# Source-stationary one-hot touches in a two-layer graph network, with their sums written straight into the layer-1 weight buffers

## The chip, the cores and the metric

The program runs on one core of a Trainium2 chip. The metric is the device time of one execution in microseconds (us), the median of three runs. The core has a matrix engine (PE; PEld is its weight load, which can run beside a matmul), a vector engine (DVE), a scalar engine (ACT), GpSimd (POOL) and a queue engine that issues transfers (SP). On-chip memory (SBUF) has 128 partitions; matmuls write into PSUM, from which ACT or DVE must carry the sums away.

## What is computed

The graph has 2500 nodes and 80000 edges, sorted by target node `dst`; the density of edges falls with the row, since `dst` is drawn as 2500 u². Rows have 1024 columns, all in float32. Two layers follow one another:

```
h = relu(layernorm(x))
s = h @ W0
x = x + segment_sum(s[src] * edge_weight[:, None], dst)            # first graph layer

h = relu(layernorm(x))
g = h @ W1.T + b
row, col = dst and src, with one self loop for each node
deg = number of edges of each row (self loop included)
norm = deg[row] ** -0.5 * deg[col] ** -0.5
out = x + segment_sum(norm[:, None] * g[col], row)                 # second graph layer
```

## The kernel before

Gathers and segment sums are done as dense matmuls. For each tile of 128 target rows the kernel builds a 2500-wide matrix of summed edge weights (20 blocks of 128 sources), and for the second layer a matrix of edge counts. A float32 factor is carried as two float16 parts (high, low), and a product as the three products (0,0), (0,1), (1,0) of parts.

**Touches.** The matrices come from one-hot products. A touch is one matmul over 128 consecutive edges: its stationary side is a one-hot of 128 columns, its moving side a one-hot of the rest of the address, three times (plain, times the weight's high part, times its low part). DVE builds both from fields that POOL copies (L989, L991, L994, L995); eight touches are one step. A window is 4 target rows; four windows are a quad (16 rows), eight quads a tile, 160 quads in all. Before, the stationary side is (row in the window, source block), 4 x 32 = 128 columns, and the moving side the position in the source block, 80 columns times three = 240. Quads 0 to 15 (two tiles) take as many touches as the edges need (352 in 44 steps); quads 16 to 63 take two touches for each window (8 for a quad, 384 in all), quads 64 to 159 one (4 for a quad, 384 in all). A window with edges left over gets further touches; with the edges drawn there are none, before or after.

**Stages.** First the *support* stage: 20 tiles of `h @ W0` (L1634), with transposes (L1617), tables that find each window's edges (L1703) and the touches of the first 16 quads in between. Then the *dense* stage of layer 1: 20 tiles, each 120 matmuls of 512 columns (L1750), cut into eight parts of 15 by `SUMS_AT`; ahead of each part PE does the touches (L1646) of one quad of the tile **two** further on. The last two dense tiles run with no touches. Then layer 2, five chunks of 500 columns: 320 matmuls against the counts (L1846), then four products with `W1` (L1902, 48 matmuls each).

**A quad's way out, before.** ACT makes three copies out of PSUM (L1380 to L1382: the counts in float32, the weights' high part, the low sums); DVE forms the low part (`second_part`, L1054 and L1057); SP stores both parts in DRAM (`store_quad`, L471), ACT's own queue stores the counts (L1384), POOL adds them to a running degree (L741). When a tile's eight quads are stored, SP loads the tile back turned round (`load_weights`, L484, four transposing DMAs of 10 blocks of 128 x 128), two tiles ahead of their use. The counts come back in float32 (`load_counts`, L554); POOL adds the self loops (L787), ACT takes the high part (L1532) and DVE the low (L1221). The degree is summed by PE (L1826) and turned by a DRAM round trip and two PE transposes (L1832, L1833).

**What sets the order.** Each engine has its own program, written out by hand, and waits on semaphores. `win_act`, `win_evac` and `win_lo` say that a quad's ACT copies, the PSUM release and the low part are done, `win_sum` that its counts are added, `agg_ready` that a dense tile is finished. POOL's copies of fields (L734, L735) wait for `hots_ready`, the end of DVE's previous step. SP's queue is in order: a wait there holds all transfers behind it.

## Time and profile before

| | us |
|---|---|
| median of 3 runs | 1483.26 (1482.24 to 1484.04) |
| span of the profiled execution | 1480.6 |
| around the span, to the median | 2.7 |
| PE busy | 1444.0 (98%) |
| DVE / ACT / POOL busy | 958.5 / 441.1 / 303.0 |
| dense matmuls L1750, 2400, busy | 542.2 |
| touches L1646, 1120, busy | 144.2 |
| layer-2 sums L1846, 1600, and products L1902, 960, busy | 339.1 and 209.0 |

A matmul's busy time counts its whole way through a pipelined engine, and matmuls overlap; a group's price is therefore read from the start of one group to the start of the next in the timeline. The chain of waits says which engine the end of the program hangs on. A DMA issue on SP lasts as long as the row says before the next item of SP's queue can go, and lands later.

### The profile page before, as it was taken

Reading aid. Unit: us, or ns where it says so; the run is one execution under the profiler, and the core shown is the slowest. Engines: PE = TensorE matmul, PEld = TensorE weight load, DVE = VectorE, ACT = ScalarE, POOL = GpSimd, SP = SyncE. Lnnn points to the kernel's source line nnn. Section 1 sums busy time; section 2 is a strip of 40 time slices with the busy share of each in tenths; the row PEclk is TensorE's granted clock in tenths of the full one; section 3 lists DMA queues with packets and bytes.
Section 4 is the critical chain, followed back from the end, with each engine's and each line's share of the span. In section 5 each row is a group of like instructions: output and inputs, shape, how many; then the busy total and the mean of one; then the engine's idle time right before and its main releaser. Section 6 shows DMA issues by size and latency. Waiting matters only on the chain.

```text
span 1480.6 us, 24633 instructions
## 1 busy us (share of the span) xinstructions
PE 1444.0 (98%) x7580; PEld 766.2 (52%) x7581; DVE 958.5 (65%) x1732; ACT 441.1 (30%) x869; POOL 303.0 (20%) x578
## 2 busy tenths in 40 slices
PE   3989999999999999999999999999999999999999
PEld 2555555555555555555555544446446446446455
DVE  7788785767877866666665634986554554555542
ACT  7545554422222223322223313812011011021000
POOL 2244333323333333333333310000000000001000
PEclk9999999999999999999999999999999999999999
DMA  8301431237667788888888886804305105104002
GB/s 310 115 24 47 123 102 24 46 80 146 156 149 154 160 180 186 175 182 181 179 183 181 180 181 227 282 29 150 102 8 183 61 18 185 49 29 140 28 1 83
DMA packets 414350, 185.62 MB, mean 125 GB/s; under 512 B 379624, under 2 KB 396540, under 8 KB 414216
## 3 DMA queue, kind: packets, MB, share of 16 engines
q1 hardware_dynamic: 329736, 157.82, 42.0%
q10 hardware_dynamic: 84480, 26.22, 7.2%
q8 instruction: 59, 0.97, 0.3%
q14 instruction: 75, 0.61, 0.2%
HBM read 76.45 MB, written 77.11 MB: 104 GB/s over the span
## 4 chain that ended last, share of the span: by engine, by line
PE 87%; DVE 7%; DMA 2%; issue 2%; ACT 1%; SPq 1%; DVEq 0%; POOL 0%; ACTq 0%; POOLq 0%
PE pair L1750 28%; PE pair L1846 22%; PE pair L1902 13%; PE pair L1634 13%; PE pair L1646 7%; PE pair L1703 1%; PE pair L1617 1%; DVE slots L994 1%; DVE slots L995 1%; DMA h<-x_scratch 1%; DVE negbase L1316 1%; DMA wstage<-c_scratch 1%; DVE slots L989 0%; SPq L484 0%; DVE slots L991 0%
## 5 line engine op out<-in xcount | busy, mean ns | idle before, releaser
L1750 PE MATMUL pair<-h,area 128*128 128x512 f16 x2400 | 542.2, 379 | 0.5 <-issue 0.5
L1750 PEld LDWEIGHTS pair<-h,area 128*128 128x128 f16 x2400 | 233.8, 98 | 252.5 <-issue 2.2
L1846 PE MATMUL pair<-area,h 128*128 128x500 f16 x1600 | 339.1, 374 | 1.3 <-DVE h L1250 1.3
L1846 PEld LDWEIGHTS pair<-area,h 128*128 128x128 f16 x1600 | 155.5, 97 | 184.0 <-issue 2.2
L741 POOL TENSOR_TENSOR deg_acc<-deg_acc,area 128x320 f32<-128x320 f32 x160 | 151.8, 949 | 363.1 <-ACT area L1382 363.1
L1902 PE MATMUL pair<-wmat,area 128*125 128x512 f16 x960 | 209.0, 379 | 0.0
L1380 ACT ACTIVATE area<-pair 128x320 f32<-128x320 f32 x160 | 70.1, 438 | 425.2 <-PE pair L1646 416.6
L1902 PEld LDWEIGHTS pair<-wmat,area 128*125 128x125 f16 x960 | 130.6, 136 | 75.5
L1054 DVE SCALAR_TENSOR_TENSOR area<-pair,area 128x320 f16<-128x320 f32 x160 | 77.6, 485 | 133.6 <-ACT area L1382 112.1
L1646 PE MATMUL pair<-slots 128*128 128x240 f16 x1120 | 144.2, 267 | 7.2 <-DVE slots L995 6.1
L1646 PEld LDWEIGHTS pair<-slots 128*128 128x128 f16 x1120 | 108.8, 98 | 54.2 <-DVE slots L995 11.0
L1564 ACT ACTIVATE area<-pair,sc 128x500 f16<-128x500 f32 x40 | 27.1, 677 | 364.8 <-PE pair L1846 364.8
L1634 PE MATMUL pair<-wmat,agg_t 128*128 128x512 f16 x480 | 112.2, 384 | 3.1 <-DVE wmat L890 3.1
L1301 DVE SCALAR_TENSOR_TENSOR area<-pair,sc,area 128x500 f16<-128x500 f32 x40 | 29.3, 737 | 131.1 <-ACT area L1564 131.0
L1634 PE MATMUL pair<-wmat,xt 128*128 128x512 f16 x480 | 110.7, 382 | 0.0
L989 DVE TENSOR_TENSOR slots<-iota_r,fbuf 128x640 f16<-128x640 f16 x141 | 74.4, 528 | 49.5 <-PE pair L1646 19.6
L991 DVE TENSOR_TENSOR slots<-iota_r,fbuf 128x1024 f16<-128x1024 f16 x141 | 96.3, 683 | 0.0
L1057 DVE TENSOR_TENSOR area<-area 128x320 f16<-128x320 f16 x160 | 78.7, 492 | 5.5
L995 DVE TENSOR_TENSOR slots<-slots,fbuf 128x640 f16<-128x640 f16 x141 | 80.5, 571 | 0.0
L994 DVE TENSOR_TENSOR slots<-slots,fbuf 128x640 f16<-128x640 f16 x141 | 78.0, 553 | 0.0
L1634 PEld LDWEIGHTS pair<-wmat,agg_t 128*128 128x128 f16 x480 | 46.9, 99 | 54.3 <-issue 6.3
L1634 PEld LDWEIGHTS pair<-wmat,xt 128*128 128x128 f16 x480 | 46.7, 99 | 51.7 <-issue 1.8
(240 smaller groups left out, 1171.6 us busy)
## 6 DMA issues: line engine op xcount, KB each, us to landing
c_scratch<-area ACTq DMA_DIRECT2D x160, 160.0 KB, 3.0
a_scratch<-area SPq DMA_DIRECT2D x320, 80.0 KB, 2.4
xt<-in_x SPq DMA_DIRECT2D x19, 512.0 KB, 3.9
x_scratch<-xt SPq DMA_DIRECT2D x19, 512.0 KB, 3.4
xt<-x_scratch SPq DMA_DIRECT2D x20, 448.0 KB
out_x<-xt SPq DMA_DIRECT2D x19, 448.0 KB
wstage<-c_scratch SPq DMA_DIRECT2D x17, 500.0 KB, 4.2
slots<-c_scratch SPq DMA_DIRECT2D x17, 500.0 KB, 5.4
```

The lines of the kernel that those rows point to most:

```text
L741: pool.tensor_tensor(deg_acc[:], deg_acc[:], c_stage(s), ALU.add).then_inc(win_sum, 1)
L989: nc.vector.tensor_tensor(part(hot(s), M0, SB), columns(8, SB), by_touch(s, 1, 8, SB), ALU.is_equal).then_inc(hots_plain, 1)
L991: nc.vector.tensor_tensor(part(hot(s), 0, P), columns(8, P), by_touch(s, 0, 8, P), ALU.is_equal)
L994: nc.vector.tensor_tensor(part(hot(s), W0C, SB), part(hot(s), M0, SB), by_touch(s, 2, 8, SB), ALU.mult)
L995: nc.vector.tensor_tensor(part(hot(s), W1C, SB), part(hot(s), M0, SB), by_touch(s, 3, 8, SB), ALU.mult).then_inc(hots_ready, 1)
L1054: nc.vector.scalar_tensor_tensor(a_stage(s)[:, 1], sums[:, :, SB:2 * SB], A_DOWN, a_stage(s)[:, 0], ALU.mult, ALU.subtract).then_inc(win_e ...
L1057: nc.vector.tensor_tensor(a_stage(s)[:, 1], a_stage(s)[:, 1], a_stage(s)[:, 2], ALU.add).then_inc(win_lo, 1)
L1634: last = pe.matmul(dest[:, half * H:(half + 1) * H], h_t(t)[:, q, k, :], wmat[:, r, k, half * H:(half + 1) * H], start=k == q == r == 0, s ...
L1646: return pe.matmul(dest, touches[:, t, 0:P], touches[:, t, P:CS], start=first, stop=last, skip_group_check=True)
L1750: last = pe.matmul(sum_pair(e)[:, half * H:(half + 1) * H], wts(e)[:, q, k, :], hpart(k, r)[:, half * H:(half + 1) * H], start=k == q == r ...
L1846: ins = pe.matmul(sums_of(c, f), hpart(k, q)[:, f * P:(f + 1) * P], counts, start=first and q == 0, stop=last and q == 1, skip_group_check ...
L1902: last = pe.matmul(out_pair(m)[0:RW, half * H:(half + 1) * H], agg_of(k, q)[:, b * RW:(b + 1) * RW], wmat[:, r, k, half * H:(half + 1) * H ...
```

## The change

The two sides of a touch change places. The stationary side becomes the one-hot of the source's position in its block of 128, and the moving side (row in the window, source block of 20), times three: 120 columns for a window of 2 rows, 240 for a window of 4. Quads 0 to 63 get eight windows of 2 rows, quads 64 to 159 four windows of 4. There are 384 touches (48 steps) for the first 16 quads and 384 for quads 16 to 63, all of 120 columns, then 384 of 240.

The sums now lie with the source position on partitions, as the dense matmuls want their stationary side. ACT and DVE write them directly into the weight buffer of the next tile (`quad_of`); there the block index k runs fastest, so that one stationary operand, `wts(e)[:, q, :, k]`, takes every 20th float16 (40 bytes apart). Only the first two tiles are still parked in DRAM (`park_quad`, `fetch_parked`). The touches run one tile ahead of the dense part instead of two: dense tile 0 and tile 19 run with no touches, and a tile's dense part waits for all its quads (`win_lo`). `SUMS_EARLY` makes the first seven parts of a tile 13 or 14 matmuls and the last 25.

The counts are split at once: POOL adds the self loop into each quad (`add_self`), ACT takes the high part (`counts_first`, now in each quad), POOL the low part (`counts_left`). SP stores both as float16 (`store_counts`), and layer 2 loads them turned round by transposing DMAs, five of 16 blocks and two of 40 blocks of 128 x 128 for each chunk. The degree is reduced by DVE (`deg_turned`), with no PE part. `V_HALF` grows from 288 or 192 extra columns to two halves of 384 in the window tables.

```
         def wts(b):
...
-            return area[:, b * T * P:(b + 1) * T * P].bitcast(f16).rearrange("p (q k d) -> p q k d", q=2, k=T)
+            return area[:, b * T * P:(b + 1) * T * P].bitcast(f16).rearrange("p (q d k) -> p q d k", q=2, k=T)
...
+        SUMS_EARLY = [0, 14, 27, 41, 54, 68, 81, 95, 120]
...
-                nc.vector.tensor_tensor(part(hot(s), M0, SB), columns(8, SB), by_touch(s, 1, 8, SB),
+                n = r * T
+                nc.vector.tensor_tensor(part(to, P, n), columns(8, n), by_touch(s, 0, 8, n),
...
+            def add_self(n, s, td, q):
+                pool.wait_ge(more_consts, 3)
+                pool.wait_ge(win_sum, n + 1)
+                own = by_source(c_stage(s))[:, bass.ds(td, 1), :]
+                pool.tensor_tensor(own, own, half_ident[:, q * RQ:(q + 1) * RQ].unsqueeze(1), ALU.add).then_inc(c_self, 1)
+
+            def counts_left(n, s, first_parts, second_parts):
+                pool.wait_ge(c_hi, n + 1)
+                pool.tensor_tensor(second_parts, by_source(c_stage(s)), first_parts, ALU.subtract).then_inc(c_lo, 1)
...
-                need(act, st_out[s], STORED(n, s))
-                need(act, win_sum, n - 1)
+                need(act, c_lo, n - 1)
+                need(act, win_lo, n - 1)
...
+            def counts_first(n, s, to):
+                act.wait_ge(c_self, n + 1)
+                act.activation(to, by_source(c_stage(s)), ACT.Copy).then_inc(c_hi, 1)
...
+            def store_counts(td, b):
+                sp.wait_ge(c_lo, QPT * td + QH * (b + 1))
+                for z in range(2):
+                    sp.dma_start(c_rows[z][:, :, bass.ds(at, QH * RQ)],
+                                 c_half(b)[:, z]).then_inc(c_out[b], 16)
+
+            def load_first_parts(c, j):
+                at = slice(HK * j, HK * (j + 1))
+                sp.dma_start_transpose(ct_hi[:, at, :], c_dram[0, c * CW:c * CW + CP2, HK * j * P:HK * (j + 1) * P]).then_inc(
+                    cthi_in[j], 16)
...
+            sp.wait_ge(agg_ready, T - 1)
+            sp.wait_ge(win_lo, NQ)
+            sp.wait_ge(c_out[0], 32 * (PQ + T - PRE))
+            sp.wait_ge(c_out[1], 32 * (T - PRE))
+            for j in range(HJ):
+                load_first_parts(0, j)
             store_x1(last, 0)
...
+                    if c + 1 < NCK and b == 0:
+                        sp.wait_ge(agg2_ready, KD * (c + 1))
+                        sp.wait_ge(acc_ready, c + 1)
+                        for j in range(HJ):
+                            load_first_parts(c + 1, j)
+                        for j in range(LJ):
+                            load_second_parts(c + 1, j)
...
                 if g == 0:
+                        pe.wait_ge(win_lo, QPT * (td + 1))
                     pe.wait_ge(x1_ready, td - 1 + X1_FROM)
-                    last = pe.matmul(sum_pair(e)[:, half * H:(half + 1) * H], wts(e)[:, q, k, :],
+                    last = pe.matmul(sum_pair(e)[:, half * H:(half + 1) * H], wts(e)[:, q, :, k],
```

**Where instructions move.** POOL, the loop of the dense stage, before: what stands there for one quad (L734 and L735 copy the fields of the next step, L741 adds the counts).

```order
L734 COPY fbuf<-area 128x32
L735 ISA
L735 COPY fbuf<-own_w 128x32
L397 REGISTER_ALU [waits win_act]
L741 TENSOR_TENSOR deg_acc<-deg_acc,area 128x320 [waits win_sum]
```

The same place after; L771 and L772 are the two copies, L778 the sum, L785 the self loop, L790 the low part.

```order
L771 COPY fbuf<-area 128x32
L772 ISA
L772 COPY fbuf<-own_w 128x32
L776 REGISTER_ALU
L778 TENSOR_TENSOR deg_acc<-deg_acc,area 128x320 [waits win_sum,win_act]
L785 ISA [waits win_sum,more_consts]
L785 TENSOR_TENSOR area<-area 128x16
L790 TENSOR_TENSOR aux<-area,aux 128x20x16 [waits c_hi]
```

Two operations have come into POOL's loop behind the sum, the second with a wait for ACT; the copies for the next step stand behind both.

SP, from the end of the dense loop to layer 2's loads, before (a_scratch holds the parts of weights, c_scratch the counts, x_scratch layer 1's output).

```order
L484 DMA_TRANSPOSE area<-a_scratch 128x10x128 [waits agg_ready,st_out1,st_out0]
L484 DMA_TRANSPOSE area<-a_scratch 128x10x128 x3
L519 DMA x_scratch<-xt 128x1024 [waits x1_ready]
L526 DMA xt<-in_x 68x1024 [waits stats_ready,x1_out1]
L554 DMA wstage<-c_scratch 128x2x500 [waits hots_ready,win_sum]
L554 DMA slots<-c_scratch 128x2x500
L577 DMA deg_scratch<-agg_s 32x80 [waits degrow_ready]
L580 DMA agg_s<-deg_scratch 20x128 [waits deg_out]
```

The same place after.

```order
L519 DMA c_scratch<-aux 128x20x64 [waits c_lo]
L519 DMA c_scratch<-aux 128x20x64
L549 DMA_TRANSPOSE wmat<-w_scratch 128x8x128
L578 DMA_TRANSPOSE area<-c_scratch 128x4x512 [waits c_out0,c_out1,win_lo,agg_ready]
L578 DMA_TRANSPOSE area<-c_scratch 128x4x512 x4
L554 DMA x_scratch<-xt 128x1024 [waits x1_ready]
L588 DMA h<-x_scratch 128x4x1024 [waits sup_free,x1_out1,x1_out0]
L588 DMA h<-x_scratch 128x4x1024 [waits sup_free]
L621 DMA deg_scratch<-deg 128x20x1 [waits deg_ready]
L624 DMA deg<-deg_scratch 125x20x1 [waits deg_out]
```

Five transposing loads of the first chunk's counts now stand ahead of the store of x1 and of layer 2's first load of it, and their wait names the last dense tile but one (`agg_ready`) and the last stores of counts (`c_out0`, `c_out1`).

## Rows read from the trace of the kernel before

**Rows 1.** The page: engines' busy time; shares of the chain; POOL's busy tenths.

```profile
PE 1444.0 (98%) x7580; PEld 766.2 (52%) x7581; DVE 958.5 (65%) x1732; ACT 441.1 (30%) x869; POOL 303.0 (20%) x578
...
POOL 2244333323333333333333310000000000001000
...
PE 87%; DVE 7%; DMA 2%; issue 2%; ACT 1%; SPq 1%; DVEq 0%; POOL 0%; ACTq 0%; POOLq 0%
```

**Rows 2.** Timeline, one quad with 8 touches: start, duration, engine, line, operation.

```profile
396.00 0.98 PE L1646 MATMUL pair<-slots 128*128 128x240 f16 x8
...
396.82 3.40 PE L1750 MATMUL pair<-h,area 128*128 128x512 f16 x15
...
397.02 0.44 ACT L1380 ACTIVATE area<-pair 128x320 f32<-128x320 f32 x1 [2.96 <-PE pair L1646]
...
398.20 0.91 POOL L741 TENSOR_TENSOR deg_acc<-deg_acc,area 128x320 f32<-128x320 f32 x1 [2.72 <-ACT area L1382]
...
399.78 0.49 DVE L989 TENSOR_TENSOR slots<-iota_r,fbuf 128x640 f16<-128x640 f16 x1 [0.48 <-POOL fbuf L735]
...
400.06 0.98 PE L1646 MATMUL pair<-slots 128*128 128x240 f16 x8
```

**Rows 3.** Timeline, one quad with 4 touches.

```profile
860.72 0.57 PE L1646 MATMUL pair<-slots 128*128 128x240 f16 x4
...
861.13 0.59 PE L1750 MATMUL pair<-h,area 128*128 128x512 f16 x2
```

**Rows 4.** Timeline, 16 matmuls of 128 columns, each with its own weights.

```profile
245.17 1.06 PE L1617 MATMUL pair<-ident_u,xt 128*128 128x128 f16 x16
...
246.07 0.81 PE L1634 MATMUL pair<-wmat,agg_t 128*128 128x512 f16 x3
```

**Rows 5.** Groups by line and shape: count, busy us, mean ns, idle before.

```profile
L1750 PEld LDWEIGHTS pair<-h,area 128*128 128x128 f16 x2400 | 233.8, 98 | 252.5 <-issue 2.2
...
L741 POOL TENSOR_TENSOR deg_acc<-deg_acc,area 128x320 f32<-128x320 f32 x160 | 151.8, 949 | 363.1 <-ACT area L1382 363.1
...
L1532 ACT ACTIVATE area<-wstage 128x500 f16<-128x500 f32 x34 | 19.1, 610 | 64.5 <-POOLq L789 54.5 <-DVEq L1321 10.0
...
L1455 ACT ACTIVATE etab<-pair 128x625 f32<-128x625 f32 x4 | 5.7, 1498 | 0.0
```

**Rows 6.** Timeline, ten matmuls of the window tables, and what follows them.

```profile
238.76 1.39 PE L1703 MATMUL pair<-area 125*128 125x288 f16 x10
...
239.99 0.60 PE L1634 MATMUL pair<-wmat,xt 128*128 128x512 f16 x2
```

**Rows 7.** Groups by line and shape: an integer operation on the starting chain.

```profile
L844 DVE TENSOR_SCALAR area<-area 125x640 int32<-125x640 int32 x1 | 0.5, 495 | 0.0
```

**Rows 8.** Busy time in six stretches of 32 us from 328 to 520, summed.

```profile
sum 192.00, PE 190.23 PEld 103.26 DVE 154.67 ACT 51.43 POOL 63.19; mean PE 31.71 PEld 17.21 DVE 25.78 ACT 8.57 POOL 10.53
```

**Rows 9.** Timeline from the last touches to layer 2's first sums.

```profile
868.42 13.11 PE L1750 MATMUL pair<-h,area 128*128 128x512 f16 x60
...
873.55 7.21 SPq L484 DMA_TRANSPOSE area<-a_scratch  x4
...
921.98 3.41 PE L1750 MATMUL pair<-h,area 128*128 128x512 f16 x15
...
925.22 1.01 PE L1846 MATMUL pair<-area,h 128*128 128x500 f16 x4
```

**Rows 10.** Chain of waits: layer 2's first load, then products and sums of chunks.

```profile
910.06 10.91 DMA h<-x_scratch
...
1105.08 10.36 PE pair L1902 x48
...
1147.34 67.63 PE pair L1846 x320
```

**Rows 11.** ACT's queue: packets, MB, share of 16 engines; transposing loads: us to landing.

```profile
q10 hardware_dynamic: 84480, 26.22, 7.2%
...
area<-a_scratch SPq DMA_TRANSPOSE x80, 3.9
```

976 lines of the change are left out of this document (475 added, 501 removed).

## The prediction

> **What bounds the kernel now.** I read the page's busy shares and the chain of waits first. PE is busy 98% of the span and carries 87% of the chain; no other engine carries more than 7% [rows 1]. So the time falls only by what PE no longer does, and grows by what PE must newly wait for. Then the timeline, stage by stage. In an early quad PE goes from 8 touches to 15 dense matmuls and back with no hole: touches at 396.00, dense from 396.82, the next touches at 400.06 [rows 2]. Hence 8 touches of 240 columns cost 0.82 us, 102.5 ns each; the late quads agree, 4 in 0.41 [rows 3]. The 15 dense matmuls take 3.24, or 216 ns each [rows 2]. Two places are not full. Of 192 us among the early quads PE works 190.23 [rows 8], and from the last touches to layer 2 the 255 matmuls from 868.42 to 925.22 need 255 x 0.216 = 55.1 of 56.8 [rows 9]. Last I looked at what the others do beside PE: POOL works two to four tenths of each slice up to layer 2, and then almost nothing [rows 1].
>
> The profiled span is 1480.6 and the median 1483.26, so 2.7 us lie around the span. The sum is made on the span, and 2.7 are added.
>
> **1. Touches.** Removed: 352 early and 384 later touches of 240 columns, 736 x 102.5 ns = 75.4 us. Added: 384 + 384 of 120 columns. The 384 touches of the late quads keep 240. For 120 columns the nearest row is 16 matmuls of 128 columns with a weight load each, from 245.17 to 246.07: 56.3 ns [rows 4]. So 768 x 56.3 = 43.2, and **-32.2 us**. Bounds: halving 102.5 gives 51 ns and -36; if each touch had to wait for its whole weight load of 98 ns [rows 5], 75.3 and nothing gained. I take 56.3, since it is the same form, nearly the same width, and has 98 ns loads too.
> The Trainium skill speaks against that price: *TensorE: Matmul & The Clock Gate*, section "Back-to-back issue gap", gives about 81 ns for a sustained stream of weight load and 128-column matmul. By that, 768 x 81 = 62.2, a gain of 13 in place of 32. The row shows 56.3 in this kernel, for 16 in a row; the touches come eight in a row.
>
> **2. Window tables.** Ten matmuls of 288 columns go from 238.76 to 239.99, 123 ns each, 0.427 ns a column [rows 6]. Before there are 100 of 288 columns and 25 of 192 (82 ns): 14.3 us. After, 100 of 384 (164 ns): 16.4. With two more matmuls for the row constants and longer copies behind them I take **+3** (0 to +5).
>
> **3. End of the dense stage.** PE loses the degree matmul, two transposes and the pauses round them; the hole of 56.8 - 55.1 bounds it: **-1.5**. The degree goes to DVE and a DRAM round trip that is needed only later.
>
> **4. Start.** Two integer operations of some 0.495 us leave DVE's chain ahead of the tables [rows 7]: **-1**.
>
> **5. DVE's stalls among early quads.** One-hots shrink from 640 to 320 elements an operation for the moving side, so the lost 1.8 us of 192 [rows 8], which run over the first 48 quads, should go: **-2** (0 to -3).
>
> **6. A longer chain on POOL.** Before, POOL adds the counts (0.91, from 398.20) and its two copies are done when DVE starts at 399.78: 0.67 after the sum's end [rows 2]. After, three more links follow the sum: the self loop (128 x 16, an estimated 0.25 to 0.35 by size), a wait for ACT's high part, and the low part (320 elements, like the sum: 0.86 to 1.2). ACT reads with a step of 80 bytes. Its rows give 610 ns for 500 contiguous elements and 1498 for 625 with such a step on the write side [rows 5], about double an element; so 320 elements cost 0.44 [rows 2] to 0.9. Behind POOL's wait stand the copies for the next step, then DVE's one-hots, then PE's touches. A turn of that loop: copies 0.5, sum 0.9, self 0.3, ACT 0.6 to 0.95, low part 0.9 to 1.2, some 0.1 to 0.3 of handing over: 3.5 to 3.95. PE's own turn is 120 x 0.216 + 64 x 0.056 = 29.5 us a tile, 3.69 a quad, but 3.35 for the first seven and 5.9 for the last. So in the 48 early quads POOL and PE are about equal, and the longer last slot catches POOL up. Lost: 0 to 0.6 a quad, I take 0.2, **+10** (0 to +30). In the 96 late quads the turn is 3.65 as before (860.72 and 15 matmuls [rows 3]) and POOL copies only in every second: covered.
>
> **7. The turn to layer 2.** Before, what gates the first sums is the load of x1: issued at 910.06, 10.9 us to its first use [rows 10], sums at 925.22 [rows 9]. After, five transposing loads stand ahead of it on SP. Count from the end of dense tile 18; PE then has tile 19, 25.9 us. The last counts are stored in runs of 128 bytes, 5120 packets. The ACT queue's 84480 packets took 7.2% of 16 engines' span, 20 ns of an engine each [rows 11]: 5120 x 20 / 16 = 6.4, done at about +7. The loads have 80 blocks; four of 10 blocks took 7.21 [rows 9], 0.18 a block, so 14.4 us. Then x1's store and the 10.9 of its load: sums start at +34 to +35, PE is free at +25.9, and the 1 to 2 us that it waits now go: **+8**. Bounds: 0 if the queue's issue runs ahead of the transfers, +30 if the transposes take twice as long.
>
> **8. Layer 2.** Products of a chunk last from 1105.08 to 1147.34, 42.3 us [rows 10]. Its next counts, 160 blocks, are issued in that time: 28.8. The stores of rows behind them on SP come late by as much, but a product waits only for the row two before it, and after four of them 67 us of sums follow. **0**. The strided dense weights: a load of 98 ns lies under a matmul of 216, with 252.5 us of idle weight loading in 2400 [rows 5]; a doubled load of 196 is still hidden. **0**. The parked stores of the first 16 quads and the saved DMAs of the rest were never on the path.
>
> **Sum:** -32.2 + 3 - 1.5 - 1 - 2 + 10 + 8 = -15.7, span 1464.9, time **1467**.
>
> **Rivals.**
> *A, the forecast*, terms 6 and 7 anywhere between a little and their middle bounds: 1452 to 1480. Chance 0.53.
> *E, no new wait at all*: -33.7, so 1450. For it: POOL's turn begins below PE's, and SP may issue ahead. Chance 0.14.
> *B, POOL becomes the bound.* If POOL's low part and ACT's high part both pay double for the 80-byte step, as ACT does in its row [rows 5], the turn is 4.7 early and about 4.2 late: 48 x 1.0 + 96 x 0.55 = +100 at worst. It costs from about 3.7 a turn on; half of that loss, in place of the 10 of term 6, gives 1467 + 40 = 1507, slower. Against it: sums of 320 elements on POOL already take 0.86 to 0.95 with no step [rows 5], as if not bound by the reads. Chance 0.13, of which half ends near no change.
> *D, transposes at half speed.* A single load of 10 blocks took 3.9 from issue to landing [rows 11] in place of 1.8. At 0.36 to 0.39 a block, 160 blocks are 57 to 62 a chunk against 42 + 8 (the sums ask for the last part only after 19 blocks): the turn loses 14 more, chunk 1 18, three chunks 8 each. +56: 1523. It is slower from about 1.35 times the price on. Chance 0.11.
> *C, the strided weight load shows.* At three times 98 ns it no longer fits under 216: 2400 x 78 = +187, 1654. The threshold is 2.2 times. No row has a strided weight load; ACT's step costs about double. Chance 0.06.
> The Trainium skill bears on C: *Advanced Engine Details and Errata*, section "SBUF Cachelines", says that reads which never hit the same 16-byte line twice pay a penalty, and 40 bytes apart is such a read. It gives no size, and no row of before shows one.
> *T, touches bound by weight loads*, at 81 to 98 ns: 1486 to 1500. Chance 0.03, since the transposes run at 56 [rows 4].
>
> **How the numbers follow.** A measurement of this kernel tells about 0.2% from no change, 3 us: 1480.3 to 1486.2. Faster is A and E, 0.67. Same is half of B's chance, 0.06. Slower is the rest of B, D, C and T: 0.27. The predicted time is A's, 1467. The range must leave out no more than 2 in 10: C, D and B's far end stay outside; it goes from 1446 (E with touches at 51 ns) to 1500 (B's near end, T). A's own range is 1452 to 1480.
>
> **What would show it.** Touches: 8 in about 0.45 us from start to start; over 0.6 speaks for T. Dense: 14 matmuls in 3.02; more is C. POOL: the start of the next copies behind the low part; if PE's touches wait for DVE and DVE for POOL in most early quads, by over 0.5, it is B. The turn: a hole of PE between the last dense matmul and the first sum of about 9 us, ended by the load of x1 behind the transposes. Layer 2: chunks in 109.9 us as before; a hole ahead of sums is D. The forecast is wrong if the hole at the turn is over 25, if the late quads are longer than 3.65, or if a wait stands in the support stage, where POOL gets more small copies for the early windows and the split counts ahead of them.

## The result, and the profile after

The changed kernel takes 1524.86 us (median of 4 runs, 1522.76 to 1526.98), against 1483.11 for the kernel before on the same chip: a ratio of 1.0282, 95% interval 1.0267 to 1.0296. It is slower by 41.7 us; the forecast was 1467, and the range ended at 1500. The profiled span went from 1480.6 to 1523.2.

The page of the changed kernel, its lines on busy shares, the 40 slices of PE and POOL, and the chain that ended last:

```profile
PE 1436.6 (94%) x7586; PEld 845.3 (55%) x7587; DVE 912.0 (60%) x1644; ACT 522.7 (34%) x922; POOL 522.6 (34%) x1025
...
PE   3989999999889899999999999899999999999999
...
POOL 2246664625556666666666661000000000000000
...
PE 41%; issue 20%; POOL 16%; DVE 8%; ACT 4%; DMA 4%; POOLq 3%; SPq 2%; ACTq 2%; DVEq 0%
```

Against [rows 1], POOL's busy time went from 303.0 to 522.6, and PE carries 41% of the chain where it carried 87%. POOL is busy in only six slices of ten and is nevertheless on the path: it is a link in a loop, not a full engine. So the question is which stretches have PE waiting. Busy time by engine in three stretches, the kernel before first (support stage, early quads, late quads; the columns are the stretch and its length, then each engine's busy time and its instructions):

```profile
84.00:324.00 240.00, 235.09 (x1502) 136.29 (x1501) 176.47 (x357) 113.29 (x189) 87.23 (x181) 0.99 0.25 63
...
600.00:860.00 260.00, 260.00 (x1355) 132.50 (x1354) 165.50 (x324) 77.73 (x213) 85.22 (x144) 1.00 0.84 179
```

and the same stretches of the kernel after, with that of the early quads ([rows 8] has it before):

```profile
84.00:324.00 240.00, 224.44 (x1501) 119.64 (x1500) 178.35 (x369) 124.31 (x194) 139.34 (x351) 0.98 0.32 61
328.00:520.00 192.00, 173.45 (x989) 113.29 (x988) 118.45 (x250) 75.34 (x156) 105.92 (x192) 0.99 0.37 72
600.00:860.00 260.00, 254.28 (x1305) 173.09 (x1304) 176.15 (x310) 134.17 (x276) 162.50 (x278) 1.00 0.47 87
```

PE's idle time went from 4.9 to 15.6 us in the support stage, from 1.8 to 18.6 among the early quads, and from nothing to 5.7 among the late ones; and no other engine is near full in any of them.

By stage, from the starts of PE's groups in both timelines, beside what the terms of the forecast give for that stage:

| stage | forecast | measured | how it is measured |
|---|---|---|---|
| support, to the first dense matmul | -12.5 | +1.4 | 322.74 to 324.14 |
| dense stage, to its last matmul | -11.2 | +24.2 | 925.22 to 950.83, less 1.4 |
| hole ahead of the first sums | +8 | +7.05 | the idle time before 957.88 |
| layer 2 | 0 | +9.9 | the rest of 42.6 |
| sum | -15.7 | +42.6 | spans |

Not all of it is waiting. In three stretches of 12 us of the support stage the changed kernel's granted clock (the third column from the right) is below full speed, in the kernel before in one; first the kernel before, then the changed one:

```profile
96.00:108.00 12.00, 9.06 (x51) 5.20 (x50) 11.21 (x21) 2.18 (x5) 7.54 (x14) 0.86 0.19 58
```

```profile
84.00:96.00 12.00, 8.97 (x65) 5.09 (x64) 9.48 (x34) 6.41 (x9) 2.37 (x12) 0.86 0.01 2
96.00:108.00 12.00, 8.93 (x68) 5.02 (x66) 10.79 (x24) 2.08 (x5) 9.07 (x21) 0.84 0.14 45
108.00:120.00 12.00, 12.00 (x77) 6.23 (x76) 8.51 (x16) 5.35 (x6) 6.11 (x11) 0.88 0.05 15
```

Within them the clock is at 0.50, the lower of its two levels (1.2 of 2.4 GHz), for about 3 us from 91 and about 6 from 105, both times after PE had stood idle. PE's busy time, taken in stretches of 1 us, times the share of the clock that was missing gives an estimate of what this cost: 4.6 us in the support stage (1.7 before), 1.6 in the dense stage (none before) and 4.9 at the turn to layer 2 (none before). So about 9 of the 42.6 us are the lower clock behind PE's holes; the rest is the holes themselves, less what the narrower touches save.

The loop that holds PE in the early quads: one turn in the changed kernel's timeline (start, duration, engine, line, tiles; in brackets the idle time before it and what ended it). L771 and L772 are POOL's copies of the fields, L778 its sum of counts, L785 the self loop, L790 the low part, L1410 ACT's high part, L1042 DVE's first one-hot, L1682 the touches:

```profile
473.77 0.99 POOL L790 TENSOR_TENSOR aux<-area,aux 128x320 f16<-128x320 f32 x1 [0.97 <-ACT aux L1410]
...
474.71 0.21 POOL L771 COPY fbuf<-area 128x32 f16 x1
474.85 0.21 POOL L772 COPY fbuf<-own_w 128x32 f16 x1
...
475.07 0.87 POOL L778 TENSOR_TENSOR deg_acc<-deg_acc,area 128x320 f32<-128x320 f32 x1
475.10 1.02 DVE L1042 TENSOR_TENSOR slots<-iota_r,fbuf 128x320 f16<-128x320 f16 x1
...
476.10 0.71 POOL L785 TENSOR_TENSOR area<-area 128x16 f16 x1 [0.16 <-POOL deg_acc L778]
...
476.84 0.86 ACT L1410 ACTIVATE aux<-area 128x320 f16<-128x320 f32 x1 [1.85 <-POOL area L785]
...
477.27 0.59 PE L1682 MATMUL pair<-slots 128*128 128x120 f16 x8
...
477.78 0.97 POOL L790 TENSOR_TENSOR aux<-area,aux 128x320 f16<-128x320 f32 x1 [0.97 <-ACT aux L1410]
...
479.16 1.02 DVE L1042 TENSOR_TENSOR slots<-iota_r,fbuf 128x320 f16<-128x320 f16 x1 [1.18 <-POOL fbuf L772]
```

From one low part to the next are 4.01 us, and within them POOL waits only 0.97 for ACT and some tenths in handing over. PE's touches follow POOL's copies, and POOL's next sum follows the touches: PE's quads take 3.8 to 4.65, and the last of a tile 6.31. A tile of 8 early quads takes 35.04 to 35.44 (34.55 and 36.49 once each) where PE's own work is 29.5; a late tile 29.96 to 30.34 (29.18 before).

More of PE's idle time among these quads lies between the touches and the dense matmuls behind them, ended by nothing that the profile shows (11.9 us in 27 places from 350 to 530), than ahead of the touches, ended by DVE (6.1 in 7). These gaps belong to the loop too: they are 0.5 in the kernel before, and 1.7 in e11 below, whose quads have the same instructions on PE.

At a tile's end something else shows, in the same timeline:

```profile
526.99 0.86 ACT L1410 ACTIVATE aux<-area 128x320 f16<-128x320 f32 x1 [4.87 <-PE pair L1783]
...
527.93 0.95 POOL L790 TENSOR_TENSOR aux<-area,aux 128x320 f16<-128x320 f32 x1 [4.00 <-ACT aux L1410]
```

ACT's wait for the tile's last dense matmul (`agg_ready`) stands ahead of the high part of the tile's last quad, and POOL, with the next copies behind its own wait, stands still for 4.0 us just when it should have caught up.

The turn, in the chain of waits of the changed kernel (start, duration, what):

```profile
946.42 24.29 DMA deg_scratch<-deg
...
976.67 17.68 DMA x_scratch<-xt
...
1007.26 5.00 DMA area<-in_L_gnn_b
...
1012.80 0.75 DVE own_w L1350
```

and PE at the same place, from its timeline:

```profile
957.88 28.60 PE L1870 MATMUL pair<-area,h 128*128 128x500 f16 x128 [7.05 <-DVE h L1287]
987.48 27.15 PE L1870 MATMUL pair<-area,h 128*128 128x500 f16 x128 [0.99 <-DVE h L1287]
1017.61 15.35 PE L1870 MATMUL pair<-area,h 128*128 128x500 f16 x64 [2.98 <-issue]
1035.40 12.23 PE L1930 MATMUL pair<-wmat,area 128*125 128x512 f16 x48 [2.45 <-DVE area L1330]
```

The degree goes to DRAM as 2560 single elements, 10 KB in all, and SP stands behind it for 24.3 us. All that SP issues later is late: the other x1 tiles, the second parts, the bias, and behind the bias DVE's 40 operations of L1350 at 0.75, which the products wait for. From the first sums to the first products are 77.5 us; before they were 69.1 (925.22 to 994.36). The difference of 8.4 is 5.1 us more of holes, of which the one of 2.98 ends with nothing that the profile shows (e14 below is on it), and about 3 of lower clock: in the hole of 7.05 the granted clock falls to 0.50 and stays there to 960, and 128 sums take 28.60 where the next 128 take 27.15; behind the hole of 2.98, 64 sums take 15.35, against 13.67 in e3 at full clock.

### The profile page after: what moved, and what is told of

It reads as the page before. It is cut to its first block, busy times and chain, and to the rows that moved or that the text cites. A ratio compares the mean times of both kernels' runs of the same rounds, so it can differ in the third digit from the quotient of the medians.

```text
span 1523.2 us, 24189 instructions
## 1 busy us (share of the span) xinstructions
PE 1436.6 (94%) x7586; PEld 845.3 (55%) x7587; DVE 912.0 (60%) x1644; ACT 522.7 (34%) x922; POOL 522.6 (34%) x1025
## 4 chain that ended last, share of the span: by engine, by line
PE 41%; issue 20%; POOL 16%; DVE 8%; ACT 4%; DMA 4%; POOLq 3%; SPq 2%; ACTq 2%; DVEq 0%
PE pair L1870 18%; PE pair L1930 13%; POOL deg_acc L778 7%; PE pair L1783 5%; PE pair L1670 4%; POOL area L785 3%; DVE own_w L1350 2%; ACTq L1397 2%; DMA deg_scratch<-deg 2%; POOLq L757 1%; ACT area L1404 1%; DMA x_scratch<-xt 1%; ACT area L1405 1%; POOL fbuf L760 1%; PE pair L1682 1%
## 5 line engine op out<-in xcount | busy, mean ns | idle before, releaser
L1783 PEld LDWEIGHTS pair<-h,area 128*128 128x128 f16 x2400 | 342.0, 147 | 183.1 <-issue 36.0
L1410 ACT ACTIVATE aux<-area 128x320 f16<-128x320 f32 x144 | 125.0, 868 | 268.1 <-POOL area L785 207.9
L1042 DVE TENSOR_TENSOR slots<-iota_r,fbuf 128x320 f16<-128x320 f16 (+1 forms) x145 | 101.3, 699 | 175.3 <-POOL fbuf L772 128.5
L790 POOL TENSOR_TENSOR aux<-area,aux 128x320 f16<-128x320 f32 x144 | 144.7, 1005 | 173.4 <-ACT aux L1410 173.4
L778 POOL TENSOR_TENSOR deg_acc<-deg_acc,area 128x320 f32<-128x320 f32 x160 | 144.1, 901 | 46.2 <-ACT area L1405 43.6
L1682 PE MATMUL pair<-slots 128*128 128x120 f16 (+1 forms) x1152 | 112.3, 235 | 21.0 <-DVE slots L1048 15.4
L1682 PEld LDWEIGHTS pair<-slots 128*128 128x128 f16 x1152 | 83.2, 98 | 68.5 <-DVE slots L1048 30.5
L1670 PE MATMUL pair<-wmat,aux 128*128 128x512 f16 x480 | 115.0, 389 | 3.1 <-DVE wmat L937 3.1
L1044 DVE TENSOR_TENSOR slots<-iota_r,fbuf 128x1024 f16<-128x1024 f16 x145 | 114.3, 788 | 0.0
L1403 ACT ACTIVATE area<-pair 128x320 f32<-128x320 f32 x160 | 70.0, 437 | 75.6 <-PE pair L1682 59.9
L785 POOL TENSOR_TENSOR area<-area 128x16 f16 (+1 forms) x160 | 66.2, 414 | 28.3 <-POOL deg_acc L778 24.9
L1670 PEld LDWEIGHTS pair<-wmat,aux 128*128 128x128 f16 x480 | 46.2, 99 | 53.6 <-issue 7.3
```

The source lines that it names most:

```text
L778: pool.tensor_tensor(deg_acc[:], deg_acc[:], c_stage(s), ALU.add).then_inc(win_sum, 1)
L785: pool.tensor_tensor(own, own, half_ident[:, q * RQ:(q + 1) * RQ].unsqueeze(1), ALU.add).then_inc(c_self, 1)
L790: pool.tensor_tensor(second_parts, by_source(c_stage(s)), first_parts, ALU.subtract).then_inc(c_lo, 1)
L1042: nc.vector.tensor_tensor(part(to, P, n), columns(8, n), by_touch(s, 0, 8, n), ALU.is_equal).then_inc(hots_plain, 1)
L1044: nc.vector.tensor_tensor(part(to, 0, P), columns(8, P), by_touch(s, 1, 8, P), ALU.is_equal)
L1410: act.activation(to, by_source(c_stage(s)), ACT.Copy).then_inc(c_hi, 1)
```

## The experiments

Each edit stands on the changed kernel unless another base is named. The loss is the median less that of the kernel before on the same chip, and differences below are differences of losses:

| kernel | median us | loss us | ratio, 95% interval | dense from | dense stage | hole | sums to products |
| --- | --- | --- | --- | --- | --- | --- | --- |
| the changed kernel | 1524.86 | +41.7 | 1.0282 [1.0267, 1.0296] | 324.1 | 626.7 | 7.1 | 77.5 |
| e1_act_order | 1518.85 | +36.8 | 1.0254 [1.0237, 1.0271] | 320.2 | 621.7 | 6.8 | 77.0 |
| e2_deg_queue | 1523.93 | +41.9 | 1.0281 [1.0264, 1.0298] | 323.3 | 626.1 | 20.3 | 70.0 |
| e3_pool_copies | 1509.03 | +27.0 | 1.0198 [1.0172, 1.0225] | 321.6 | 615.0 | 6.5 | 75.6 |
| e4_all_three | 1509.98 | +28.0 | 1.0186 [1.0169, 1.0203] | 324.2 | 612.1 | 18.4 | 68.9 |
| e5_copies_ahead | 1506.15 | +24.6 | 1.0179 [1.0159, 1.0199] | 320.2 | 610.3 | 6.5 | 79.1 |
| e6_low_later | 1495.99 | +14.5 | 1.0108 [1.0091, 1.0125] | 320.6 | 601.4 | 8.0 | 74.4 |
| e7_fields_first | 1499.74 | +18.2 | 1.0122 [1.0105, 1.0138] | 327.6 | 601.2 | 8.0 | 75.6 |
| e8_turn_too | 1486.15 | +4.6 | 1.0033 [1.0022, 1.0044] | 324.0 | 601.3 | none | 75.3 |
| e9_turn_alone | 1506.51 | +24.8 | 1.0171 [1.0155, 1.0187] | 320.9 | 625.9 | none | 71.7 |
| e10_sum_in_gap | 1497.58 | +15.9 | 1.0111 [1.0096, 1.0126] | 319.5 | 610.0 | 3.6 | 74.3 |
| e11_all | 1473.23 | -8.5 | 0.9941 [0.9928, 0.9955] | 321.3 | 589.1 | none | 75.2 |
| e12_degree_last | 1471.38 | -10.2 | 0.9936 [0.9923, 0.995] | 318.2 | 589.1 | none | 76.2 |
| e13_light_support | 1514.18 | +31.8 | 1.0221 [1.02, 1.0242] | 320.2 | 626.4 | 7.1 | 75.2 |
| e14_no_branch | 1463.63 | -18.8 | 0.9873 [0.9857, 0.9888] | 319.9 | 589.7 | none | 67.5 |

The last four columns are read from PE's timeline of the profiled execution, in us: when the dense stage starts, how long it lasts, the hole ahead of the first sums, and the time from the first sums to the first products (before: 322.7, 602.5, none, 69.1). The start of the dense stage moves without an edit: the code ahead of it is the same in the changed kernel, e1, e2 and e9, and it is 324.14, 320.15, 323.27 and 320.87. Part of that is the granted clock (the estimate made above gives 4.6, 3.2, 4.6 and 3.3 us for the support stage). So a few us of a difference need not come from the edit, and what an edit did to the dense stage is read from its length.

**e1_act_order: the wait at the tile's end goes behind the high part.**

```
-    if q == 0:
-        act.wait_ge(agg_ready, td)
     if q > 0 or before:
         counts_first(n - 1, ...)
+    if q == 0:
+        act.wait_ge(agg_ready, td)
```

> One edit to the changed kernel: in a tile's first slot ACT takes the high part of the last quad's counts before it waits for the dense tile (agg_ready), not after. Theory L (the loop through POOL and ACT sets the pace, and that wait stops it once a tile, so that the long last slot gives nothing back): an early tile goes from 35.0 us to the loop's own 8 x 4.0 = 32.0, a late tile from 30.25 to PE's own 29.2; over 6 early and 12 late tiles 18 + 12.6, so about 30 us less than the changed kernel, some 1495. Rival M (PE loses the time itself, in strided weight loads and in the gaps behind the touches that no engine ends): tiles stay at 35.0 and 30.25, 1525.

It takes 4.9 off, and 5.0 off the length of the dense stage. The early tiles still take 34.3 to 35.9: the first two slots of a tile go from 4.65 + 4.07 to 3.45 + 4.9, a sum of 8.35 in place of 8.7. Two quads together take at least about 8 us whatever the last slot leaves: the wait at the tile's end isn't what sets the pace.

**e2_deg_queue: the degree's two transfers issued by ACT, ahead of the turn.**

```
-    sp.dma_start(deg_dram..., deg[:, 0:T], ...)      # and its reload
+    act.wait_ge(deg_ready, 1)
+    act.dma_start(deg_dram..., deg[:, 0:T], ...)     # and its reload
```

> One edit to the changed kernel: the degree's two element-wise transfers (out to DRAM, and back) are issued by ACT instead of SP, the first as soon as the degree is there. Theory L (SP stands 24.3 us in the wait for the first of them, and holds the later loads of x1 and the second parts of the counts, which DVE needs before the second product): the hole ahead of the second product of chunk 0, and the holes in its sums, go; the start of the 144 products moves from 1049.5 to about 1040, so 9 to 10 us less. Rival N (DVE's own work of 31 us on the norms and 40 of splits is what is late, whenever the transfers come): under 3 us.

It takes nothing off. SP's issues and PE in its timeline:

```profile
934.49 19.68 SPq L578 DMA_TRANSPOSE area<-c_scratch  x5
```

```profile
969.66 70.18 PE L1869 MATMUL pair<-area,h 128*128 128x500 f16 x320 [20.25 <-DVE h L1280]
```

The later holes are gone (320 sums in one group), but the five transposing loads now take 19.68 us to issue, not 13.14, and the hole ahead of the sums is 20.25, not 7.05. The last store of counts lands in 10.28 us, not 5.36. The single elements, landing in 16.8 us here, run beside both: the loss moved ahead of the sums.

**e3_pool_copies: POOL's copies for the step after next in the gap behind the self loop, where it waits for ACT.**

```
     sum_counts(n, s)
     add_self(n, s, td, q)
+    if ahead:
+        own_step(n + 2 + PRE_STEPS - PQ, q % 2)
```

> One edit to the changed kernel: among the early quads POOL copies the fields one step further ahead, in the gap in which it waits for ACT's high part, and not after the low part. Theory L: the loop falls from 3.99 to about 3.65 a quad in seven of eight quads, 2.4 us a tile, six tiles: 14 us less. Rival M (PE's own losses): no change. Rival K (POOL and DVE hold each other up at their memory port, 1.02 in place of 0.33 us for the first one-hot operation beside POOL's sum): the loop stays near 4.0, since the same operations still meet; under 4 us.

It takes 14.7 off, 11.7 of it in the dense stage. The copies are out of the loop, yet most slots still take 3.94, since the sum has become longer; the gain lies in a tile's first two slots (3.45 and 3.24, in place of 4.65 and 4.08), where the copies no longer stand behind the wait at the tile's end. POOL in its timeline:

```profile
472.88 1.40 POOL L778 TENSOR_TENSOR deg_acc<-deg_acc,area 128x320 f32<-128x320 f32 x1
474.43 0.34 POOL L785 TENSOR_TENSOR area<-area 128x16 f16 x1 [0.16 <-POOL deg_acc L778]
...
476.81 1.40 POOL L778 TENSOR_TENSOR deg_acc<-deg_acc,area 128x320 f32<-128x320 f32 x1
```

The sum takes 1.40 in place of 0.87 and the self loop 0.34 in place of 0.71: the sum starts here with DVE's operation on 1024 elements (L1046, 472.87, 0.68 us), while in the changed kernel that operation (L1044, 476.05) lies beside the self loop.

**e4_all_three: the three edits together.** 

> The three edits together (ACT's order, the degree's transfers issued by ACT, POOL's copies in the gap). Theory L: early tiles at max(29.5, 8 x 3.65 = 29.2), so 29.5 to 30; late tiles 29.2; the turn 9 us shorter: 1525 - 32 - 12.6 - 9.5 = about 1471, faster than the kernel before. Rival M: 1515 at best.

 No better than e3 alone, far from what was expected: the dense stage is 2.9 shorter than e3's, but the hole ahead of the sums is 18.39, as in e2.

**e5_copies_ahead: e1, and the copies two steps ahead but ahead of the sum.** 

> On top of e1's order of ACT: among the early quads POOL copies the fields of the step two quads on, ahead of the sum of counts, as the first thing of its turn. e1 showed that the wait for the dense tile was not what holds the early tiles (34.8 us). Theory L2 (a chain through two quads: touches, ACT's copies, POOL's sum and self loop, ACT's high part, POOL's low part, POOL's copies, DVE's one-hots, touches of the quad after next: 8.0 us for two quads, so no slack of a long slot can be kept): with the copies ahead of the sum the chain is cut, and only POOL's own turn of 4.0 is left: early tiles at 32.0, about 16 to 18 us less than the 1518.9 of e1, some 1502. Rival K (POOL and DVE hold each other up at a shared memory port): operations still meet, early tiles 33 to 35, over 1508. Rival M (PE's own gaps): 1518.

 1506.15, somewhat above what was expected. Early tiles 32.3 to 34.7. The dense stage is 16.4 shorter than the changed kernel's.

**e6_low_later: e5, and POOL's low part one quad later, so that it waits for no one.**

```
     sum_counts(n, s)
     add_self(n, s, td, q)
-    counts_left(n, s, ...)
+    left_of(n - 1, (q - 1) % QPT)
```

> e5, and POOL takes the low part of a quad's counts one quad later, behind the next quad's sum and self loop, so that it no longer waits for ACT's high part (0.95 us a quad). Theory L2: POOL's turn falls to about 3.1 early and 2.7 to 3.1 late, under PE's 3.2 to 3.4: early tiles at PE's 29.5, late tiles at 29.2 (30.25 before): 33 + 12.6 less than the changed kernel, some 1479. Rival K: the turn stays at 3.5 or more early, tiles at 31 to 32, late tiles at 29.2 to 30: 1490 to 1500.

Another 10.1 off, less than expected. Early tiles fall to about 30.5, nearly PE's own 29.5, but late tiles now alternate between about 29.4 and 31.2. A new link has closed: the staging tile has two slots, and ACT may not write one before the low part has read it. A wait of that kind:

```profile
703.51 0.44 ACT L1411 ACTIVATE area<-pair 128x320 f32<-128x320 f32 x1 [0.42 <-POOL aux L790]
```

**e7_fields_first: e6, and in the support stage POOL's fields ahead of the counts.** 

> e6, and in the support stage POOL copies the fields of the next quad's first two steps ahead of the counts of the last quad (in the changed kernel the counts stand ahead of all fields). PE works 224.4 of 240 us there in the changed kernel and 235.1 before. Theory: the touches wait for fields behind counts: 5 to 10 us less than e6. Rival (the holes come from DVE's work for the tables and POOL's sheer load of some 40 small copies): under 2.

 A miss: 3.7 more, not 5 to 10 less, and the dense stage starts at 327.60. PE's holes that end with DVE in the support stage are no shorter (12.6 us from 84 to 324, 11.4 in e6), and the granted clock is lower there (0.96, 0.99 in e6). The order on POOL alone is not what the support stage lost.

**e10_sum_in_gap: one edit on the changed kernel. The self loop comes first and the sum of counts lies in the gap in which POOL waits for ACT** (the sum then holds the self loops; DVE no longer adds the one; in the dense stage a one-element addition on POOL, 0.18 to 0.34 us, goes ahead of the self loop).

```
-    sum_counts(n, s)
     add_self(n, s, td, q)
+    sum_counts(n, s)
```

> One edit to the changed kernel: in each quad POOL adds the self loop first and the sum of counts behind it, so that the sum (0.87 us) lies in the gap in which POOL waits for ACT's high part (0.95); the degree then holds the self loops already. ACT's order and the copies stay as in the changed kernel. Theory L2 (a chain through two quads of 8.0 us: touches, ACT, POOL, ACT, POOL, DVE, touches): the chain loses the sum, 0.9 to 1.0, and is 7.0 for two quads, 3.5 a quad against PE's 3.2 to 3.4: an early tile goes from 35.07 to 31 to 31.5, a late one to 29.2 to 29.6, so 1525 - 6 x 3.8 - 12 x 0.8 = about 1492. Rival K (the time is set by POOL and DVE meeting at a memory port): tiles at 33 or more, 1512.

It takes 25.9 off with one swap, the most of the single edits. The sum, 0.86 to 1.06 us, no longer lies between the touches and ACT's high part. The profiled execution is 28.1 shorter: 16.7 of it are the dense stage, 4.6 an earlier start of that stage (about what it moves without an edit), and 6.7 the turn. Late tiles fall to 29.6 to 29.9, early ones to 31.6 to 34.3; in the middle of a tile the slots are down to PE's own 3.45 and 3.24. Now the tile's end shows as in the changed kernel:

```profile
479.33 0.95 POOL L792 TENSOR_TENSOR aux<-area,aux 128x320 f16<-128x320 f32 x1 [3.32 <-ACT aux L1412]
```

**e9_turn_alone: one edit on the changed kernel. SP stores and loads x1 first, spreads the transposing loads between, and sends the degree last** (DVE's and ACT's work on the degree that comes back moves behind it).

```
-    ... five load_first_parts, then store_x1(last, 0), load_x1(0..3) with the degree behind load_x1(1)
+    store_x1(last, 0)
+    for k in range(4):
+        load_x1(k)
+        for j in ((0, 1), (2, 3), (4,), ())[k]:
+            load_first_parts(0, j)
+    ... second parts, bias, load_rows, then the degree and its reload
```

> One edit to the changed kernel: only the new order of SP's queue at the turn of the layers that e8 has too (x1's store and first load ahead of the transposing loads of counts, these spread among the other loads of x1, the degree's element-wise transfers last). Theory L: 7.3 us of hole ahead of the first sums and some 10 ahead of the second product go, but about 5 stay with the skip of 320 instructions in the first chunk's sums: 13 to 15 us less than the changed kernel, as between e7 and e8: about 1511. Rival N (DVE's own work sets the second product's start): 7 or less.

It takes 16.9 off. The first sums start with the last dense matmul (946.73, no hole), and the products 71.7 us later. The profiled execution is 19.0 shorter: 7.05 is the hole, 7.9 layer 2, and 4.1 lie ahead of the turn, where the code is the same. The same order on e7, as **e8_turn_too**, takes 13.6 off e7:

> e7, and at the turn of the layers SP stores x1 and loads its first part ahead of the transposing loads of counts, which are spread among the loads of x1, while the degree's element-wise transfers go behind all of them. Theory L: sums of layer 2 start when PE is free (7.3 us earlier), and the second product waits no longer for the norms (10 us): 15 to 17 us less than e7. Rival N (DVE's splits and its 31 us of norms set the second product's start, whatever the transfers do): 7 us or less.

**e11_all: e1, the copies ahead, e10 and e9 together, and the second parts of chunk 0 skipped in eight jumps over 40 instructions each, where the changed kernel has one over 320.** 

> Together: ACT's order (e1), POOL's copies two steps ahead (e5), the sum of counts in POOL's gap (e10), the turn (e8), and the skip of the second halves of counts in the first chunk's sums made in eight jumps over 40 instructions, as the kernel before has it, in place of one over 320. Theory: early tiles at PE's 29.5 (35.07), late at 29.2 to 29.5 (30.25), the turn 14 shorter, the skip 4 to 5: 1525 - 33 - 11 - 14 - 5 = about 1462 to 1465, 1.2% faster than the kernel before. If the chain through ACT still holds the late tiles (as e6's 30.3 did), 1473.

1473.23 (1471.77 to 1473.92): 0.6% below the kernel before, though not the 1462 to 1465 that was hoped for. Its three stretches:

```profile
84.00:324.00 240.00, 225.45 (x1514) 121.33 (x1512) 180.28 (x375) 125.93 (x197) 139.75 (x355) 0.99 0.33 63
328.00:520.00 192.00, 185.22 (x1113) 127.19 (x1112) 142.42 (x289) 87.30 (x179) 133.25 (x261) 1.00 0.40 77
600.00:860.00 260.00, 260.00 (x1356) 181.21 (x1354) 190.00 (x322) 139.70 (x286) 186.74 (x355) 1.00 0.50 92
```

PE is full again among the late quads (29.18 a tile, as before), early tiles take 30.0 to 31.7, and the sums start with no hole. Two things stay: the support stage (its row is nearly that of the changed kernel), and a hole behind the turn, in PE's timeline:

```profile
969.57 16.20 PE L1875 MATMUL pair<-area,h 128*128 128x500 f16 x64 [5.01 <-issue]
```

**e12_degree_last: e11, and SP stores the degree only when the second parts of chunk 0 have landed.**

```
     sp.wait_ge(deg_ready, 1)
+    sp.wait_ge(ctlo_in[LJ - 1], 16)
     sp.dma_start(deg_dram..., deg[:, 0:T], ...)
```

> The version with all four edits, and one wait more: SyncE stores the degree only when both loads of second parts of chunk 0 have landed. W (the 2560 small pieces of the degree's store delay the second parts, and the 5.0 us hole of PE ahead of its first matmul on them is that delay): the hole goes, PE runs on from about 964.5, the degree lands some 5 to 10 us later, and the time falls by 4 to 5 from 1473, to about 1468. R (the hole is PE's own, a branch and its reload): the hole stays at about 5, and the time is 1473 or a few us more. If the hole goes and the time does not fall, the degree has become what the products wait for.

Not to be told from e11. SP, behind its wait for the second parts, and PE:

```profile
945.73 0.38 SPq L658 DMA_DIRECT2D deg_scratch<-deg  x1
```

```profile
967.37 16.27 PE L1876 MATMUL pair<-area,h 128*128 128x500 f16 x64 [5.94 <-issue]
```

The second parts had landed by 945.73, and the hole runs from 961.4 to 967.4: they are not its cause.

**e14_no_branch: e11, without PE's branch to the second parts in chunk 0** (that work, which these inputs skip, is left out; the waits for the loads stay).

```
-    for f in range(KD):
-        second_halves(0, (f,))
+    for j in range(LJ):
+        pe.wait_ge(ctlo_in[j], 16)
```

> The version with all four edits, in which PE has no branch to the second parts of the counts in chunk 0 (that work, which this input's counts skip, is left out; the waits for the loads stay). R (the 5.0 us hole of PE ahead of the last four source tiles is the branch and what it takes to go on behind it): the hole goes, and the time is 1468 to 1469 against 1473. W (something else is waited for there): the hole stays at 5, and the time is 1473 (1471 to 1474).

10.3 off e11. All 320 sums run in one group:

```profile
909.60 67.63 PE L1875 MATMUL pair<-area,h 128*128 128x500 f16 x320
```

In e11 they took 75.2 from first to last, holes and jumps included; so the skipped block costs about 7.6 us there. Some 2.5 of them are the clock: behind the hole of 5.01 the granted clock is 0.50 from 968 to 974, and 64 sums take 16.20 in place of 13.67. In e10, which skips the block in one jump, 320 sums took 69.07 without a hole, and the 1.4 more than here fits the clock too, which is at 0.50 from 933 to 935 behind the hole ahead of them: there the skip costs nothing that shows. The number of jumps doesn't decide: with one jump the hole at this place is 5.17 in e8, 2.98 in the changed kernel, 2.37 in e9, 0.51 in e13, and none in e2, e4, e6 and e10. The skipped block is the place; why the hole is there in some kernels and not in others is open.

**e13_light_support: the changed kernel, with POOL's operations on the counts of the first 16 quads cut to a tenth of their width or less** (degree and low parts of these quads are left out for the rest).

> The changed kernel, with POOL's three operations on the counts of the first 16 quads (those in the support stage) cut to a tenth or less of their width: the sum to 16 of 320 columns, the low part to 1 of 20 source tiles (so the degree and the low parts of these quads are left out for the rest; the order, the waits and all stores stay). S (the support stage ends about 12 to 15 us late because POOL's longer chain for these quads, about 2.4 us each, holds back the fields, and they the one-hots): the holes of PE that end with DVE in 84 to 324 us shrink from 12.4 in all to under 6, the dense stage starts 6 to 10 earlier, at 314 to 318, and the time falls from 1525 to 1515 to 1519. D (the holes are the one-hots' and window tables' own, or ACT's): the dense stage starts within 2 of 324, and the time stays above 1522.

It takes 9.9 off (1511.73 to 1521.9). What PE waited for in the support stage (84 to 324), in the changed kernel and then in this one (total, times, longest):

```profile
PE pair L1682 <- DVE slots L1048: 8.2, 5, 3.0
PE pair L1682 <- DVE area L1110: 4.2, 3, 2.5
```

```profile
PE pair L1688 <- DVE slots L1054: 6.2, 4, 3.0
PE pair L1688 <- DVE area L1116: 2.2, 2, 1.2
```

The holes go from 12.4 to 8.4. In e1, e2 and e9, whose support stage is that of the changed kernel, they are 10.8, 11.7 and 11.4; so 2.4 to 4.0 us of the holes are the length of POOL's operations, between the two theories. What that is worth in time isn't shown: the dense stage starts at 320.20, 3.9 earlier than in the changed kernel, but e1's starts at 320.15 without the edit, at a higher clock. (The profiled run gains 2.4 more between the first sums and the first products, where its hole at the skipped block is 0.51 in place of 2.98; the rest of the 9.9 it doesn't show.) The other 8.4 us are open. One such hole in the changed kernel's timeline, seen from ACT, POOL and DVE:

```profile
200.50 0.20 ACT L1443 ACTIVATE scale<-scale 128x2 f32<-128x2 f32 x1 [3.96 <-DVE scale L867]
...
201.54 0.94 POOL L790 TENSOR_TENSOR area<-area 128x320 f16<-128x320 f32 x1 [5.70 <-ACT area L1410]
...
203.79 0.33 DVE L1042 TENSOR_TENSOR slots<-iota_r,fbuf 128x320 f16<-128x320 f16 x1 [2.38 <-POOL fbuf L762]
...
205.65 0.59 PE L1682 MATMUL pair<-slots 128*128 128x120 f16 x8 [0.93 <-DVE area L1110]
```

ACT's high part stands behind ACT's own wait for DVE (3.96), POOL's low part waits 5.70 for it, the fields stand behind that, and the one-hots behind the fields. That the wait, not the work, is the rest fits these rows, but e7, which put two steps of fields ahead of it, did not gain; it isn't shown.

## Why the prediction was wrong, point by point

**Term 1, touches: right.** Eight touches of 120 columns take 0.42 (318.12 to 318.54), 52.5 ns each, against 56.3 forecast. Rival T and the 81 ns of the Trainium skill (*TensorE: Matmul & The Clock Gate*, "Back-to-back issue gap") are not borne out: this trace disagrees. PE has less to do where the narrower touches are, as forecast; it only doesn't get to do it earlier.

**Terms 2 to 5.** The price of the window tables held: ten matmuls of 384 columns go from 193.84 to 195.47, 163 ns each, 164 forecast. Term 5 came out the other way: among the early quads the 1.8 us of idle time became 18.6. Terms 3 and 4 are too small to be told from the rest.

**Term 6, POOL's chain: the step that failed, and its size.** The term was +10. The early tiles lost 6 x 5.5 = 33 and the late ones 12 x 1.1 = 13, 46 in all, 36 more than the term: most of the miss of 58. Two sentences of the term are wrong. "The longer last slot catches POOL up": it can't. The turn is a closed loop, touches to ACT to POOL's sum and self loop to ACT's high part to POOL's low part to the copies to DVE to the touches, about 8 us for two quads. What a long slot has to spare can't be kept for the next ones, and ACT's wait at the tile's end held it there too (e1: 5 us of it). And "covered" for the late quads: with copies in every second quad there is the same loop with more slack, and it still cost 1.1 a tile, which went to 0.4 to 0.7 when e10 moved the sum out of the loop and to nothing in e11. The prices of the links:

```profile
L1410 ACT ACTIVATE aux<-area 128x320 f16<-128x320 f32 x144 | 125.0, 868 | 268.1 <-POOL area L785 207.9
...
L790 POOL TENSOR_TENSOR aux<-area,aux 128x320 f16<-128x320 f32 x144 | 144.7, 1005 | 173.4 <-ACT aux L1410 173.4
...
L785 POOL TENSOR_TENSOR area<-area 128x16 f16 (+1 forms) x160 | 66.2, 414 | 28.3 <-POOL deg_acc L778 24.9
```

(groups of the changed kernel by line: busy, mean ns of one, idle before). ACT's 868 ns lies at the upper end of the 0.6 to 0.95 given, POOL's 1005 within 0.9 to 1.2; the self loop takes 0.71 among the early quads, not 0.25 to 0.35. The turn came out at 4.0, just over the upper end of 3.5 to 3.95. So the sizes were nearly right. What was wrong was to set the turn against a tile's mean of 3.69 a quad, which lets slack of one slot pay for another. Against the seven slots of 3.35 it is 0.65 too long each, 4.6 a tile. The late quads have the same fault: 3.65 is a tile's mean there too, and their slots took 3.74 to 3.79 on the mean, one of the three signs that the prediction gave for being wrong.

**Rival B was the right mechanism with a wrong ground.** It held that POOL becomes the bound if both readers pay double for the step of 80 bytes. ACT paid, POOL did not; POOL's loop became the bound all the same. Its sign in the last part, PE on DVE and DVE on POOL by over 0.5 in most early quads, is what the trace shows (350 to 560: the weight loads of the touches wait for DVE in 33 of 48 quads, 0.59 on the mean, and DVE for POOL's copies in 35, 1.68). It had 0.13.

**The support stage: the miss that no term had.** It was named only as what would make the forecast wrong. It costs 14 (+1.4 where -12.5 was forecast). PE is idle 10.7 us longer than before, and the lower clock behind the holes costs some 3 more (4.6 against 1.7); 2.4 to 4.0 of the idle time are the width of POOL's operations (e13).

**Term 7, the turn: right in its size, for its own hole.** The first sums start 33.7 after the end of tile 18, forecast 34 to 35; the hole is 7.05, forecast 8 to 9. The five transposing loads took 13.14 to issue, 14.4 forecast; rival D is out.

**Term 8, layer 2: wrong by 9.9.** It cost the loads of counts and never the degree's round trip, which term 3 calls "needed only later". It is needed later, but it is issued early: SP stands behind it for 24.3 us, and part of the sums and the products behind SP. e9 took 16.9 us back by order alone, the hole of 7.05 and 7.9 of this. About 4.9 of the 9.9 are the lower clock behind PE's holes, which no term had, and the hole of 2.98 at the skipped block isn't the degree's. The later chunks are nearly as before, as forecast (first products 41.0 later than before, the end 42.6).

**The weight load with a step: right.** The group of dense weight loads in the changed kernel:

```profile
L1783 PEld LDWEIGHTS pair<-h,area 128*128 128x128 f16 x2400 | 342.0, 147 | 183.1 <-issue 36.0
```

147 ns, not 98 [rows 5]: the step of 40 bytes costs half as much again, and it lies under a matmul of 216, so rival C is out. The Trainium skill (*Advanced Engine Details and Errata*, "SBUF Cachelines") has such a penalty without a size; here the trace agrees with it.

One correction to the listing ahead of the prediction: in the reference's second layer `row` is `src` and `col` is `dst`, so it counts and sums over the edges of each source.

## What to carry to other kernels

When an edit adds links between engines, draw the closed loop from an operation back to its next instance, add its links one after the other, and hold the sum against the shortest slots of the bounding engine, not against their mean; an engine busy six tenths can be what all others wait for. Then look for a link that only has to happen at some time (here the sum of counts) and put it in a gap of the loop: that swap alone took 26 us of 42 back, 16.7 of them in the dense stage, as much there as the edits to waits and copies together (e5, 16.4). Cost every transfer that is moved to a shared queue by its pieces, not its bytes, even if nobody needs its data soon: what stands behind it on the queue does. And look at the granted clock behind each new hole before all of the loss is put down to waiting.

## What the runs showed of the hardware

- **POOL and DVE slow each other.** DVE's one-hot of 320 elements (L1042) takes 0.33 us alone and 1.02 beside POOL's sum, ending 0.18 after it; POOL's sum takes 0.87 at one place and 1.40 at another (e3), its self loop 0.34 and 0.71. The Trainium skill (*SBUF — State Buffer*, "SBUF: two separate sides") calls the port pair of the two an exclusive lock, in which the loser fully blocks; the first of these rows agrees with that in the main (fully blocked, the one-hot would end 0.33 after the sum, not 0.18). Moving one of them moves the wait.
- **Single elements are dear in DRAM.** 2560 pieces of 4 bytes, 10 KB, took 24.3 us to land beside the loads of x1 and 16.8 beside the store of counts and the transposing loads, which took 19.68 to issue there and 13.14 without them.
- **A skipped block can cost.** On PE the jump over it cost 7.6 us behind the turn in e11 (e14), a hole of 5.01 and lower clock behind it, and nothing that shows in e10.
- **A hole can cost more than its length.** PE's granted clock fell to 0.50 (1.2 of 2.4 GHz) in the changed kernel's hole of 7.05 and was there to 960, 2 us into the sums; in e2's hole of 20.25 it fell too and was still 0.50 at 973, and the 320 sums took 70.18 against e14's 67.63.
